# Routed experts: the first row tile gathered as quarter rows and turned in 32x32 blocks on VectorE

## The reference

```python
logits = xt @ gate_w.T
scores = jnp.sqrt(jax.nn.softplus(logits))
_, idx = jax.lax.top_k(scores + gate_b, K)
w = jnp.take_along_axis(scores, idx, axis=1)
w = w / jnp.sum(w, axis=1, keepdims=True)
...
buf = jnp.zeros((E, CAP, D)).at[e, posc].add(x_pairs)
g = jnp.einsum('ecd,eid->eci', buf, W1)
u = jnp.einsum('ecd,eid->eci', buf, W3)
h = jax.nn.silu(g) * u
out = jnp.einsum('eci,edi->ecd', h, W2)
y_pairs = out[e, posc] * (w.reshape(-1) * valid)[:, None]
...
shared = (jax.nn.silu(xt @ Ws1.T) * (xt @ Ws3.T)) @ Ws2.T
return y + shared
```

## Time and profile before

| | |
|---|---|
| Median of 3 runs | 482.31 us (482.02 to 483.34) |
| Span of the profiled execution | 480.7 us |
| Median less span (launch and end; the profiled execution's own time is not listed apart) | 1.6 us |
| PE busy | 459.8 us (96%) |
| PEld busy | 391.9 us (82%) |
| DVE busy | 329.0 us (68%) |
| ACT busy | 255.6 us (53%) |
| POOL busy | 209.6 us (44%) |
| Mean granted TensorE clock | 0.998 |
| DMA | 95.02 MB, mean 198 GB/s |

### The profile page before, as it was taken

One profiled execution on the slowest core, in us unless ns is written; L12 is line 12 of the kernel. 1 busy time (PEld: TensorE's weight loads), 2 busy tenths in 40 slices (PEclk: granted clock), 3 DMA queues, 4 the chain that ended last, 5 costly groups with the idle time before them and its releaser, 6 DMA issues.

```text
span 480.7 us, 7804 instructions
## 1 busy us (share of the span) xinstructions
PE 459.8 (96%) x2493; PEld 391.9 (82%) x2493; DVE 329.0 (68%) x724; ACT 255.6 (53%) x379; POOL 209.6 (44%) x175
## 2 busy tenths in 40 slices
PE   2899899999999999999999999999999999999994
PEld 1477777878888888888888999999999999999983
DVE  6689779998896854388649776766666766667520
ACT  4764443546554453452436576566556666666531
POOL 0513433655444365434176535444425444442242
PEclk9999999999999999999999999999999999999999
DMA  8644765666665344272469989998879998887545
GB/s 297 192 168 124 232 230 160 223 232 217 229 203 213 140 127 138 79 89 28 60 164 201 297 268 281 278 282 260 258 203 259 255 273 262 256 256 232 109 59 73
DMA packets 29164, 95.02 MB, mean 198 GB/s; under 512 B 4816, under 2 KB 5328, under 8 KB 28624
## 3 DMA queue, kind: packets, MB, share of 16 engines
q0 software_dynamic: 17040, 43.66, 37.0%
q1 hardware_dynamic: 11808, 50.98, 31.2%
q10 hardware_dynamic: 288, 0.01, 0.0%
HBM read 67.50 MB, written 28.70 MB: 200 GB/s over the span
## 4 chain that ended last, share of the span: by engine, by line
PE 87%; DVE 5%; DMA 5%; issue 1%; ACT 1%; POOL 1%; POOLq 0%; DVEq 0%
PE psG L1277 48%; PE psY L1277 28%; PE psT L1282 7%; DMA out<-xh_sb,idx 3%; PE psG L1535 1%; DMA front<-in_x,idx 1%; DMA tok_i<-in_ids 1%; PE psY L1294 1%; PE psG L1306 1%; DVE stats L929 1%; ACT front L569 1%; DVE xh_sb L902 0%; POOLq L81 0%; DVE stats L936 0%; DVE arena L907 0%
## 5 line engine op out<-in xcount | busy, mean ns | idle before, releaser
L1277 PE MATMUL psY<-arena 128*128 (+1 forms) x372 | 91.1, 395 | 1.6 <-DVE arena L907 1.6
L1277 PEld LDWEIGHTS psY<-arena 128*128 128x128 f32 x372 | 68.7, 188 | 16.4 <-issue 2.4
L498 POOL DMA_INDIRECT ht<-out,idx x32 | 33.6, 1051 | 64.9 <-PE psT L1282 49.1
L1277 PE MATMUL psY<-slot,arena 128*128 128x512 f32 x240 | 58.9, 395 | 0.0
L1052 DVE TENSOR_TENSOR slot<-raw,slot 128x1536 fp32r<-128x1536 f32 x25 | 43.9, 1757 | 19.7 <-ACT slot L624 19.6
L1277 PE MATMUL psG<-arena 128*128 x228 | 57.0, 399 | 0.0
L1052 DVE TENSOR_TENSOR arena<-raw,arena 128x1536 fp32r<-128x1536 f32 x24 | 42.0, 1758 | 17.3 <-ACT arena L624 17.3
L1277 PEld LDWEIGHTS psY<-slot,arena 128*128 128x128 f32 x240 | 44.2, 188 | 9.3 <-DVE arena L1237 0.2
L1277 PE MATMUL psG<-arena,slot 128*128 128x512 f32 x216 | 51.4, 392 | 0.0
L1277 PEld LDWEIGHTS psG<-arena 128*128 128x128 f32 x228 | 41.5, 188 | 8.6 <-issue 0.4
L1277 PEld LDWEIGHTS psG<-arena,slot 128*128 128x128 f32 x216 | 40.1, 188 | 8.2
(11 more groups left out here) (228 smaller groups left out, 801.7 us busy)
## 6 DMA issues: line engine op xcount, KB each, us to landing
raw<-in_w SPq DMA_DIRECT2D x51, 768.0 KB, 5.7
padded<-xh_sb SPq DMA_DIRECT2D x19, 256.0 KB, 2.2
raw<-in_ctx_t SPq DMA_DIRECT2D x2, 1024.0 KB, 8.7
ht<-in_ctx_t SPq DMA_DIRECT2D x1, 1024.0 KB, 11.6
xh_sb<-in_ctx_t SPq DMA_DIRECT2D x1, 1024.0 KB, 7.9
out<-log_sb SPq DMA_DIRECT2D x4, 256.0 KB, 8.1
ht<-out,idx POOLq DMA_INDIRECT x32, 4.4
xb<-in_x,idx POOLq DMA_INDIRECT x19, 4.1
```

What stands on the lines that cost most here:

```text
L498: pool.indirect_dma_start(ht[:, n, :], None, halves_of_out, slots(e * NA + a, 0)).then_inc(g_here[n], 16)
L1277: ins = pe.matmul(ps, left[a], right[b], start=n == 0 and m == 0, stop=n == total - 1 and m == 2)
```

## The change

It turns the first row tile (a = 0) of each routed expert on DVE and leaves the second (a = 1) to PE.

- The gather of tile a = 0 is four indirect DMAs, each 128 partitions by 128 numbers (512 bytes a partition). In piece j, partition p gets the quarter p // 32 of the row of token 32 j + p % 32. A new table `idxq` holds the positions of these quarter rows.
- DVE's `turn` is one instruction, a transpose in 32x32 blocks of 128x512, from `ht` into `turned`, a strip of the buffer `big` that is free by then. It reads every fourth number of a quarter row, so that position d = 4 p + k lands on partition p in chunk k. ACT and DVE then make `gl` from `turned`, in SBUF, instead of from `psT[0]`.
- PE makes four transposes for an expert instead of eight. Their input is now every fourth column of the tile, so that tile a = 1 gets the same order of positions, and `side` lays the routed experts' input weights out in that order.
- Once, before the first gather, `idxq` is made: DVE fills `turned` with 0/1 matrices from the identity, PE multiplies four of them by the even columns of the slot table (four fp32 matmuls 128x16 between `down(8)` and `down(9)`, with a wait for DVE's table), and DVE scales the result and adds the quarter's number. One small DVE instruction more stands ahead of the writes of `idx2`.
- POOL issues five gathers for an expert instead of two. `send_y2(8)` to `send_y2(10)` now stand ahead of `gather(1)` instead of behind it. The buffers of tile a = 0 come free with `turn` (`g_turned`) instead of with PE's transposes.

```diff
+        pieces_of_out = out.rearrange("t (o d) -> (t o) d", o=2 * KD)
...
+        turned = big_all[:, 3 * NJ * E2:3 * NJ * E2 + D]
...
+            def gather_rows(e):
+                n = 2 * (e % 2) + 1
+                if e >= 2:
+                    pool.wait_ge(g_ps, e - 1)
+                pool.indirect_dma_start(ht[:, n, :], None, halves_of_out, slots(e * NA + 1, 0)).then_inc(g_here[n], 16)
+
+            def gather_pieces(e):
+                n = 2 * (e % 2)
+                if e >= 2:
+                    pool.wait_ge(g_turned, e - 1)
+                for j in range(KD):
+                    pool.indirect_dma_start(ht[:, n, j * P:(j + 1) * P], None, pieces_of_out,
+                                            bass.IndirectOffsetOnAxis(ap=idxq[:, j, e:e + 1], axis=0)).then_inc(g_here[n], 16)
+
             def gather(e):
-                for a in range(NA):
-                    n = 2 * (e % 2) + a
-                    if e >= 2:
-                        pool.wait_ge(g_ps, (e - 2) * NA + a + 1)
-                    pool.indirect_dma_start(ht[:, n, :], None, halves_of_out, slots(e * NA + a, 0)).then_inc(g_here[n], 16)
+                gather_rows(e)
+                gather_pieces(e)
...
             pool.wait_ge(r2_idx, 1)
-            gather(0)
+            gather_rows(0)
+            pool.wait_ge(r2_quad, 1)
+            gather_pieces(0)
+            for j in range(2 * TB, 3 * TB - 1):
+                send_y2(j)
             gather(1)
-            for j in range(2 * TB, NJ - 2):
+            for j in range(3 * TB - 1, NJ - 2):
                 send_y2(j)
...
+            def turn(e, par, first):
+
+                n = 2 * par
+                dve.wait_ge(g_here[n], KD * landed(e, par))
+                if not first:
+                    dve.wait_ge(g_lo, (e - 1) * NA + 1)
+                dve.transpose(turned.rearrange("p (k j i) -> p k j i", k=KD, j=KD),
+                              ht[:, n, :].rearrange("p (j l k) -> p k j l", j=KD, k=KD)).then_inc(g_turned, 1)
...
             link(dve.tensor_scalar(U[1], U[3], 2.0, 2.0 * PAD + 1, ALU.mult, ALU.add))
+            dve.scalar_tensor_tensor(S(24, 2), U[0], -2.0 * PAD, U[1], ALU.mult, ALU.add).then_inc(r2_row, 1)
             link(dve.scalar_tensor_tensor(idx2[:, :, 0], U[0], -2.0 * PAD, U[1], ALU.mult, ALU.add))
...
-            hidden(10)
+            gate(10)
+            dve.wait_ge(r2_sel, 1)
+            dve.scalar_tensor_tensor(idxq[:, :, :].rearrange("p j e -> p (j e)"), psT[0][:, 0:KD * E2], float(KD),
+                                     cst[:, C_QUAD:C_QUAD + 1].to_broadcast([P, KD * E2]),
+                                     ALU.mult, ALU.add).then_inc(r2_quad, 1)
+            low(10)
             for c in range(2):
                 split(1, c, 1)
+            turn(0, 0, True)
             hidden(11)
...
                 gate_rest(1)
                 if more:
+                    turn(e + 1, 1 - r, False)
                     gate_first()
                     gathered(e + 1)
...
-            for j in range(2 * TB, 3 * TB - 1):
+            down(2 * TB)
+            pe.wait_ge(r2_row, 2)
+            rows = small[:, 24 * NJ:26 * NJ].rearrange("p (e a) -> p a e", a=NA)[:, 0]
+            for j in range(KD):
+                ins = pe.matmul(psT[0][:, j * E2:(j + 1) * E2], turned[:, j * P:(j + 1) * P], rows, start=True, stop=True)
+            ins.then_inc(r2_sel, 1)
+            for j in range(2 * TB + 1, 3 * TB - 1):
                 down(j)
...
             def gathered(e, r, first):
-                for a in range(NA):
-                    n = 2 * r + a
-                    pe.wait_ge(g_here[n], landed(e, r))
-                    if not first:
-                        pe.wait_ge(g_lo, (e - 1) * NA + a + 1)
-                    transpose4(psT[a], ht[:, n, :]).then_inc(g_ps, 1)
+                n = 2 * r + 1
+                pe.wait_ge(g_here[n], landed(e, r))
+                if not first:
+                    pe.wait_ge(g_lo, e * NA)
+                columns = ht[:, n, :].rearrange("p (c k) -> p k c", k=KD)
+                for k in range(KD):
+                    ins = pe.transpose(psT[1][:, k * P:(k + 1) * P], columns[:, k, :], ident)
+                ins.then_inc(g_ps, 1)
...
+        t[1:, :, :, :I_MLP] = routed.reshape(E2, I_MLP, P, KD).transpose(0, 2, 3, 1)
```

More of the change, by code:

```diff
@@ L58 @@
 C_RANK = C_SPARE + NQ
-C_END = C_RANK + NJ
+C_QUAD = C_RANK + NJ
+C_END = C_QUAD + 1
+QW = P // KD
 def constants():
@@ L74, in constants @@
     c[:, C_RANK:C_RANK + NJ] = np.arange(P)[:, None] + P * np.arange(NJ)[None, :]
+    c[:, C_QUAD] = np.arange(P) // QW
     return c
@@ L161, in gated_layer @@
         idx2 = sb("idx2", [P, NQ, 2], I32)
+        idxq = sb("idxq", [P, KD, E2], I32)
         w_slot = sb("w_slot", [P, NQ])
@@ L185, in gated_layer @@
         y3 = [ys, xb]
+        turned = big_all[:, 3 * NJ * E2:3 * NJ * E2 + D]
+        assert D <= 2 * NJ * E2
         onehot1 = big_all[:, 0:NJ * P // 2].bitcast(BF16).rearrange("p (b n) -> p b n", n=P)
@@ L264, in gated_layer @@
         g_here = [sem(f"g_here{n}") for n in range(4)]
-        g_ps, g_hi, g_lo = sem("g_ps"), sem("g_hi"), sem("g_lo")
+        g_turned, g_ps, g_hi, g_lo = (sem(n) for n in ("g_turned", "g_ps", "g_hi", "g_lo"))
+        r2_row, r2_sel, r2_quad = (sem(f"r2_{n}") for n in ("row", "sel", "quad"))
         up3_ps, silu3, hid3, hid3_hi, hid3_lo = (sem(n) for n in ("up3_ps", "silu3", "hid3", "hid3_hi", "hid3_lo"))
@@ L716, in gathered @@
             def gathered(e):
-                for a in range(NA):
-                    act.wait_ge(g_ps, e * NA + a + 1)
-                    act.activation(gl[0][:, :, a * P:(a + 1) * P], chunks(psT[a][:, :]), ACT.Copy).then_inc(g_hi, 1)
+                act.wait_ge(g_turned, e + 1)
+                act.activation(gl[0][:, :, 0:P], chunks(turned), ACT.Copy).then_inc(g_hi, 1)
+                act.wait_ge(g_ps, e + 1)
+                act.activation(gl[0][:, :, P:CAP], chunks(psT[1][:, :]), ACT.Copy).then_inc(g_hi, 1)
             def rows3(e, par, a, known):
@@ L1080, in hidden @@
                 low(n)
+            def turn(e, par, first):
[5 more added lines that the diff above has]
+                              ht[:, n, :].rearrange("p (j l k) -> p k j l", j=KD, k=KD)).then_inc(g_turned, 1)
             def gathered(e):
-                for a in range(NA):
+                for a, src in enumerate((turned, psT[1][:, :])):
                     dve.wait_ge(g_hi, e * NA + a + 1)
                     s = slice(a * P, (a + 1) * P)
-                    dve.tensor_tensor(gl[1][:, :, s], chunks(psT[a][:, :]), as_f32(gl[0][:, :, s]),
+                    dve.tensor_tensor(gl[1][:, :, s], chunks(src), as_f32(gl[0][:, :, s]),
                                       ALU.subtract).then_inc(g_lo, 1)
@@ L1175, in _ @@
                 hidden(8 + k)
+            dve.tensor_copy(turned.rearrange("p (j q l) -> p j q l", j=KD, q=KD),
+                            ident.rearrange("p (j l) -> p j l", j=KD).unsqueeze(2).to_broadcast([P, KD, KD, QW])).then_inc(r2_row, 1)
             dve.wait_ge(r2_src, 1)
@@ L1590, with side @@
     f = {k: np.asarray(v) for k, v in inputs.items()}
-    def side(w):
-        e = w.shape[0]
-        t = np.zeros((e, P, KD, IP), w.dtype)
-        t[:, :, :, :I_MLP] = w.reshape(e, I_MLP, KD, P).transpose(0, 3, 2, 1)
+    def side(shared, routed):
+        t = np.zeros((E2 + 1, P, KD, IP), routed.dtype)
+        t[0, :, :, :I_MLP] = shared.reshape(I_MLP, KD, P).transpose(2, 1, 0)
+        t[1:, :, :, :I_MLP] = routed.reshape(E2, I_MLP, P, KD).transpose(0, 2, 3, 1)
         return t
@@ L1604, in down @@
         return t.reshape(e, NI, P, D).transpose(0, 2, 1, 3).reshape(e, P, NI * D)
-    w1 = side(np.concatenate([f["L0_ffn_Ws1"][None], f["L0_ffn_W1"]]))
-    w3 = side(np.concatenate([f["L0_ffn_Ws3"][None], f["L0_ffn_W3"]]))
+    w1 = side(f["L0_ffn_Ws1"], f["L0_ffn_W1"])
+    w3 = side(f["L0_ffn_Ws3"], f["L0_ffn_W3"])
     w1[0, :, :, I_MLP:I_MLP + E2] = f["L0_ffn_gate_w"].reshape(E2, KD, P).transpose(2, 1, 0)
```

## The result

The change makes the kernel slower: **487.66 us** (median of four runs, 487.55 to 489.27) against 482.16 (four runs on the same chip, 481.34 to 483.34). The ratio is 1.0117, with an interval of 1.0101 to 1.0133. The forecast was 477.0, at most 483.0.

A forecast was written before the change was run, and what follows sets the result against it. The prediction took PE, busy without gaps in stage 3, to bound the kernel. Its terms, -7.0 + 0 + 1.1 + 0.3 + 0.3 = -5.3 us, turned 482.3 into 477.0 us, with a range from 475.5 to 483.0.

The forecast's parts named there:

- Transposes removed, -7.0: PE in stage 3: four transposes fewer in each of 16 experts, 64 x 0.109 us, 7.0 us less.
- stride: PE's remaining transposes read every fourth number; the longer load was taken to cost 0.
- the rival's 5.8 to 7.4: Rival of strided loads on PE: the 64 transposes cost 5.8 to 7.4 us more in all; chance 0.19.
- the 190 ns: Sign that the forecast is right: the stride leaves the PEld record of a transpose below 190 ns.
- `turn`, hidden: DVE's turn in each step takes 1.0 us, hidden by 1.9 us idle ahead of `gate_first`.
- Select, 1.1: At the border, PE's four fp32 matmuls for the table, eight passes: 1.1 us more.
- "Cost 0" for POOL: Three more gathers a step, 3.9 us: POOL uses 11.1 of 12.75 us, later adds hidden, cost 0.
- The rival on POOL: Pieces of 1.6 us each make POOL's step 13.5 of 12.75 us; kernel 481 to 485; chance 0.04 with DMA.
- The lead: POOL's gathers run some two steps ahead of their use, so later gathers and adds are hidden, cost 0.
- The border, 0.3 + 0.3: PE's waits at the border: 0.3 us for `turn(0)` and 0.3 for a late ACT in the first step.
- a stall at the border: Rival: pieces land late under load, 8.4 us, and PE waits 4.0 us instead of 0.3: 480.7; chance 0.13.
- DMA, 0: DMA engines: 384 more rows a step, 0.12 us, share rising from 0.89 to about 0.93, cost 0.

The follow-up runs named there:

- e8: The change with both drains moved from the steps to POOL's wait for the routing table, and `turn(0)` put between `gate(11)` and `low(11)`: 484.85 us.
- e7: The kernel before, with tile a = 0 filled by four gathers of 32 whole rows each: 490.16 us, ratio 1.0143.
- e3: The kernel before, with only the gather of tile a = 0 split into four quarter-row pieces: 493.69 us, ratio 1.0223.
- e1: The change, with tile a = 0 gathered by one DMA of whole rows instead of four pieces: 478.26 us, ratio 0.9915.
- e10: The change, with DVE's weight splits from expert 1 on taking their second operand from PSUM: 480.75 us, ratio 0.9968.
- e9: e12 with gathers four experts ahead instead of five and the last `send_y2` ahead of `gather(3)`: 480.18 us, ratio 0.9971.
- e12: e8 with the drain behind expert 12 put back: 484.69 us, ratio 1.0043.

## Why the prediction was wrong

- **Transposes removed, -7.0: held in the steps.** Steps of 12.79 us for a forecast of 12.75. The **stride** cost 0.8 us in all where 0 was taken, far from the rival's 5.8 to 7.4. The load record passed the 190 ns that were named as its limit (210), and PE still lost nearly nothing.
- **`turn`, hidden: held in the steps.** 1.12 us for 1.0, with 0.87 us idle left ahead of `gate_first`; only where the splits came late (386.74) is nothing left.
- **Select, 1.1: about held** (eight passes in 0.8 to 1.0 us).
- **"Cost 0" for POOL: this is the step that failed.** The count said 11.1 of 12.75 us a step, and that nobody waits. Two things were missing. First, the 2.53 us of one gather and the 2.42 of an add were taken as they stood, without asking what ran beside them. They are issues that began inside a weight split; before, the gathers lay mostly clear of the splits, and the adds that met one had idle time behind them. Pieces took 1.6 us when they met one. The rival on POOL used just this number (1.6 each) and then was given 0.04, with "nothing in the rows asks for it": the stretched rows did. Second, the price was looked for at gathers that come late for PE. It came at the adds, which stand behind the gathers in the same queue and at the end of the kernel are a chain of 8 us a pair. With 25 of 53 pieces held by a split, a step took 12.81 us of POOL where 11.1 were counted and 12.75 were there. The first pair started a step late, and the tail paid for it: +7.7 us, of which the drain behind expert 12 makes some 2.
- **The lead:** gathers 1 to 4 were costed by what they add to a step. All of them stand ahead of `add(0)`, which started at 298.86 instead of 285.69.
- **The border, 0.3 + 0.3: undersized, 3.1 instead of 0.6.** The last piece's issue began in a split (2.31 us instead of 0.99), and the wait fell on DVE ahead of the whole chain to the first step. The rival "a stall at the border" named the place and the sign; it put the cause mostly in the wrong place, on a long landing, where it was a long issue. (The count there starts `down(12)` at 253.2; the row has 253.44.) e8 gets 2.8 us back by moving `turn` alone.
- **DMA, 0: held** in the steps, as far as e7 against e3 can show; the share stayed at 0.89 where 0.93 was expected.

That the pieces cause the loss is shown (e1, e3), that POOL pays by the issue and not by the row is shown (e7), and so are the contention (e10) and that the order at the start decides between the two rhythms (e9 against e12). Why a late POOL settles at PE's step, and what the closing drain works off, stay open.

## What to carry to other kernels

Price an engine that only issues DMAs by its issues, and look at what stands behind them in its queue up to the last instruction: a queue that is late by a step costs nearly nothing until the program ends, and then much of it (7.7 us here, for adds that were 13 to 16 us late). When a few instructions of a kind are twice as long as the rest, find out what ran beside them before adding more of them; a median hides a collision that a new phase will make regular. And keep a wait of some us a step on such an engine: it is what sets its phase and what absorbs a stop.

## What the runs showed of the hardware

- An indirect DMA's issue occupies POOL for 0.91 us with 32 rows and 0.94 to 0.99 with 128, plus 0.30 to the next; with an add, 1.54 to 1.62.
- An issue that begins while a DVE instruction with two SBUF operands runs (1.76 us here) ends 0.81 to 0.85 us behind that instruction's end, an adding one 1.43 to 1.50: it becomes 1.3 to 2.3 us and up to 3.1. One that begins just ahead isn't held. With one operand in PSUM it isn't held either (e10: 0.98 us in the mean of 56 pieces of the steps, beside splits of the same 1.75 us).
- A weight load of every fourth fp32 column takes 210 ns where a packed one takes 141, and four transposes 0.49 us instead of 0.44.
- A 32x32 block transpose of 128x512 fp32 on DVE, read at a stride of four, takes 1.12 us (median 1120 ns).
- `drain` on POOL with gathers under way leaves it idle for 8.1 (before) to 10.4 us (e3); leaving the late one out costs 3 to 4 us behind the last add.
